# A two-layer MetaFormer block on one core: three stages in one arena, nine places of sixteen reused, 7 MB of a weight loaded in stage 1

## What is computed

```python
xn = layer_norm(_ln_c(x), norm_a, norm_b)
left  = (xn @ Wl + bl) * sigmoid(xn @ Wlg + blg)
right = (xn @ Wr + br) * sigmoid(xn @ Wrg + brg)
out_gate = sigmoid(xn @ Wog + bog)
out = einsum('bkjd,bkid->bijd', left, right) / n        # one 384x384x384 product per channel
x = x + (layer_norm(out, on_a, on_b) * out_gate) @ Wo + bo
t = tokens(x); u = _ln_t(t)
probs = softmax(u @ gate_w.T + gate_b, axis=tokens)      # 64 experts
topv, topi = top_k(probs per expert, 8)                  # 512 picks
pooled = sum over 8 picks of topv * u[topi]
h = gelu([pooled, 1] @ weight1)                          # weight1: 64 x 129 x 512
out = [h, 1] @ weight2                                   # weight2: 64 x 513 x 128
t = t + scatter_add(topi, out * topv)
```

## Time and profile before

| | before |
|---|---|
| median of three runs | 2838.45 us |
| the profiled execution, device time | 2838.67 us |
| its span, first to last instruction | 2836.9 us |
| busy in the span: PE / DVE / ACT / POOL | 2606.5 / 2388.4 / 2266.2 / 1822.3 us |
| moved by DMA | 872.97 MB, mean 308 GB/s |
| mean granted clock of TensorE | 0.979 of full speed |

### The profile page before, as it was taken

The page is one execution under the profiler, slowest core; times in us unless marked ns, Lnnn a source line. Parts: engine busy times, 40 slices in busy tenths (PEclk is TensorE's granted clock), DMA queues, the critical chain, the costliest instruction groups (busy, mean ns, idle before and its releaser), DMA issues. The chain is left out here.

```text
span 2836.9 us, 65594 instructions
## 1 busy us (share of the span) xinstructions
PE 2606.5 (92%) x15074; PEld 2134.2 (75%) x15074; DVE 2388.4 (84%) x4702; ACT 2266.2 (80%) x4430; POOL 1822.3 (64%) x1935
## 2 busy tenths in 40 slices
PE   7999999999999999899999999588899999999845
PEld 6888888888888888899999999466666666666623
DVE  6777777777777777899999999888988888898872
ACT  6888888888888888788888888578888888888840
POOL 7888888888888887200000000289999999899941
PEclk9999999999999999999999999799999999999977
DMA  5777777777777776999999999599999999999997
GB/s 196 271 271 271 270 268 270 268 266 267 270 271 270 271 269 251 339 347 352 349 348 349 349 349 350 186 362 342 344 356 349 351 350 350 344 352 346 348 336 239
DMA packets 280206, 872.97 MB, mean 308 GB/s; under 512 B 28286, under 2 KB 80656, under 8 KB 280176
## 3 DMA queue, kind: packets, MB, share of 16 engines
q1 hardware_dynamic: 276640, 871.37, 85.3%
q10 hardware_dynamic: 2896, 0.70, 0.1%
q0 software_dynamic: 640, 0.54, 0.1%
HBM read 492.97 MB, written 379.52 MB: 308 GB/s over the span
## 5 line engine op out<-in xcount | busy, mean ns | idle before, releaser
L1350 PE MATMUL banks<-x_parts,w_parts 128*128 128x512 f32 x4320 | 1067.3, 398 | 3.4 <-POOL x_parts L643 3.4
L1350 PEld LDWEIGHTS banks<-x_parts,w_parts 128*128 128x128 f32 x4320 | 791.2, 188 | 165.3 <-POOL x_parts L643 3.8
L1385 PE MATMUL banks<-left_parts,right_parts 128*128 128x384 f32 x3456 | 633.2, 340 | 21.3 <-ACT arena L881 10.2
L1385 PEld LDWEIGHTS banks<-left_parts,right_parts 128*128 128x128 f32 x3456 | 596.0, 188 | 58.3 <-issue 39.5
L1027 DVE SCALAR_TENSOR_TENSOR arena<-banks,cols,arena 128x512 f32<-128x512 f32 x576 | 406.4, 747 | 247.3 <-ACT arena L845 243.5
L946 ACT ACTIVATE work<-arena,rs 128x128 f32<-128x128 f32 x1152 | 354.4, 391 | 134.7 <-POOL rs L731 134.7
L692 POOL DMA_DIRECT2D coef<-yt x3 | 1.5, 517 | 656.2 <-DVE yt L1079 656.2
L1418 PE MATMUL banks<-wo_sb,arena 128*128 128x128 f32 x2304 | 395.0, 300 | 2.1 <-DVE arena L1146 2.1
L705 POOL TENSOR_TENSOR arena<-arena,work 128x512 f32<-128x512 f32 x288 | 359.9, 1271 | 56.7 <-DVE arena L1135 56.5
L1418 PEld LDWEIGHTS banks<-wo_sb,arena 128*128 128x128 f32 x2304 | 362.4, 193 | 35.6 <-POOL arena L705 2.9
L643 POOL TENSOR_TENSOR x_parts<-xn,x_parts 128x512 fp32r<-128x512 f32 x288 | 371.4, 1290 | 6.6 <-ACT x_parts L833 6.6
(11 more groups left out here) (209 smaller groups left out, 4270.9 us busy)
## 6 DMA issues: line engine op xcount, KB each, us to landing
arena<-in_x_dram SPq DMA_DIRECT2D x144, 512.0 KB, 3.4
left_d<-arena SPq DMA_DIRECT2D x144, 512.0 KB, 2.6
right_d<-arena SPq DMA_DIRECT2D x144, 512.0 KB, 3.4
gate_d<-arena SPq DMA_DIRECT2D x144, 512.0 KB, 4.2
arena<-right_d SPq DMA_DIRECT2D x128, 576.0 KB, 6.8
arena<-left_d SPq DMA_DIRECT2D x128, 576.0 KB, 7.9
mixed_d<-arena SPq DMA_DIRECT2D x128, 576.0 KB, 8.4
work<-mixed_d SPq DMA_DIRECT2D x144, 512.0 KB, 4.8
```

What stands on the lines that cost most here:

```text
L1350: last = nc.tensor.matmul(ps[2 + k][:, :], w_parts[:, wq, k], x_parts[:, xq, b, c], start=((wq, xq) == TERMS[0]), stop=((wq, xq) == TERMS[ ...
L1385: last = nc.tensor.matmul(ps[NT * b + t][:, 0:GRID], lr_parts[RIGHT][:, rq, b, k, t * P:(t + 1) * P], lr_parts[LEFT][:, lq, b, k], start=( ...
```

## The change

Stages 1 and 2 now lie over each other (`used[0]` is set back, so `rch2`, `lch2`, `mix` and `mixsq` take the words of x, signs, left, right and gate), within places 0 to 8; an assertion holds them there. `late_arena` moves to places 2 and 3. Places 9 to 15 are free from the start: SP loads each of these seven between two pieces of stage 1's loop, which has now eight pieces. Behind stage 3 SP loads places 4 to 8, and 2 and 3 after the last stores and transposes. ACT waits for all stores of gate before stage 2, since `mix` lies over their buffers. In stage 3 ACT's `copy_transposed` comes ahead of `normalise`.

```diff
         gate_sb = carve("b n", b=2, n=2 * CHUNK)
+        wcat = carve("k d", k=5, d=DIM)
+        used[0] = 4 * NT * GRID
+        rch2 = carve("b t n", b=2, t=NT, n=GRID)
         lch2 = carve("b t n", b=2, t=NT, n=GRID)
-        rch2 = carve("b t n", b=2, t=NT, n=GRID)
         early_words = arena[:, 0:4 * NT * GRID].rearrange("p (k b t n) -> p k b t n", k=2, b=2, t=NT)
         mix = carve("b t n", b=2, t=NT, n=GRID)
         mixsq = carve("b t n", b=2, t=NT, n=GRID)
-        wcat = carve("k d", k=5, d=DIM)
-        newton = carve("t n", t=NT, n=GRID)
         sum1 = carve("t n", t=NT, n=GRID)
         sum2 = carve("t n", t=NT, n=GRID)
+        newton = carve("t n", t=NT, n=GRID)
         rstd_map = carve("t n", t=NT, n=GRID)
...
-        assert used[0] <= W1_WORDS
+        PLACE = BANDS * HIDDEN
+        FIRST_FREE = 9
+        LATE_PLACES = (2, 3)
+        assert used[0] <= FIRST_FREE * PLACE
...
-        late_arena = arena[:, W1_WORDS - 8 * CHUNK:].rearrange("p (k b h n) -> p k b h n", k=2, b=2, h=2)
+        late_arena = arena[:, LATE_PLACES[0] * PLACE:LATE_PLACES[0] * PLACE + 8 * CHUNK].rearrange("p (k b h n) -> p k b h n", k=2, b=2, h=2)
...
-            pairs(sp, STEPS, stage1)
+            w1_view = weight1[:, 0:DIM, :].rearrange("(g j) p n -> j p g n", g=BANDS)
+
+            def load_w1(j):
+                sp.dma_start(w1_sb[:, j], w1_view[j]).then_inc(s_w1[j // 2], 16)
+
+            pairs(sp, STEPS, stage1, cuts=[lambda j=j: load_w1(j) for j in range(FIRST_FREE, SIDE)])
...
-            def load_w1(n):
-                for j in range(2 * n, 2 * n + 2):
-                    sp.dma_start(w1_sb[:, j], w1_view[j]).then_inc(s_w1[n], 16)
...
                     if isinstance(j, int) and 4 * j + r == STEPS - 2:
                         load_w1(0)
+                        load_w1(1)
...
-            for n in range(1, WLOADS - 1):
-                load_w1(n)
+            for j in range(LATE_PLACES[-1] + 1, FIRST_FREE):
+                load_w1(j)
...
-            load_w1(WLOADS - 1)
+            for j in LATE_PLACES:
+                load_w1(j)
...
+            for b in range(2):
+                act.wait_ge(s_gst[b], 16 * (STEPS // 2))
             high_halves(0, 0)
             quads(act, DIM, stage2, drain=1)
...
                         exponentials(*shifted(i, b, -4))
+                    if in_range(i, b, -2, STEPS):
+                        copy_transposed(*shifted(i, b, -2))
                     if in_range(i, b, -1, STEPS):
                         normalise(*shifted(i, b, -1))
-                    if in_range(i, b, -2, STEPS):
-                        copy_transposed(*shifted(i, b, -2))
```

More of the change, by code:

```diff
@@ L551, in store_result @@
                 sp.dma_start(out[s], late_arena[:, 1, b].rearrange("p h (c d) -> p (h c) d", c=TILES)).then_inc(s_ost[b], 16)
-            w1_view = weight1[:, 0:DIM, :].rearrange("(g j) p n -> j p g n", g=BANDS)
-            def load_w1(n):
-                for j in range(2 * n, 2 * n + 2):
-                    sp.dma_start(w1_sb[:, j], w1_view[j]).then_inc(s_w1[n], 16)
             def stage3(j):
```

## The result

The change takes **2821.61 us** (median of five runs, 2820.62 to 2821.97) against 2836.05 us for the kernel before in the same session (2833.65 to 2839.62): ratio 0.9947, interval 0.9932 to 0.9961. It is faster by 0.5%, some 15 us, where the prediction had 58 and its range ended at 2815.

What follows compares the result with a forecast made beforehand. A dependency loop among the engines in stage 3, 12.16 us per two steps, was taken as the bound, not the transfers. 2838.7 - 48.9 - 2.2 - 7.3 = 2780.3, so 2780 us; range 2758 to 2815.

Steps and rivals of the forecast that it cites:

- What is late next? I take the floors of a step one by one: Stage 3, loop broken: separate floors for engines, buffers and DMA; the buffer loop was taken as binding, 5.75 us a step.
- The term of 48.9 us: Stage 3: copy before normalise saves 0.357 us in each of 137 steady steps, reaching 5.75 us a step.
- a 12 us pair that remains: Stage 3: a sign that would show the forecast wrong, two steps still taking about 12 us.
- POOL's floor, 5.58: Stage 3: POOL's least time per step, 731.4 us busy over 131 steps, 5.58 us.
- The buffer floor of 5.68: Stage 3: a gate buffer's round of issue, landing, DVE and POOL takes 11.35 us in two steps, 5.68 each.
- The end of stage 3, -2.2: End of stage 3: with the copy first, the last logits start 2.2 us sooner.
- The gather, -7.3: After stage 3: with seven fewer weight loads there, the gather lands after 4.5 us instead of 11.78, saving 7.3 us.
- C: Stage 3 rival, chance 0.12: another way of the same length replaces the loop, only the tail gains; 2829 us, or 2836.
- B: Stage 3 rival, chance 0.20: the transfers are the wall, DVE's L1135 waits for gate loads; 2794 to 2821 us.
- D: Stage 3 rival, chance 0.04: slower, ACT's new transposes wait adds to its root wait; 6.7 us a step, 2911 us.
- E: Stage 1 rival, chance 0.04: the seven early loads stall it, with A elsewhere; 2780 + 19 = 2799 us.
- A: The main case, chance 0.60: the loop breaks, a stage 3 step takes 5.62 to 5.85 us; 2758 to 2795 us.

Runs made afterwards that it cites:

- e1: The change with the old order on ACT, normalise ahead of copy_transposed: 2828.95 us.
- e8: e5 with the old order on ACT, normalise ahead of copy_transposed: 2823.33 us.
- e3: The change, but DVE scales and adds the first tile of a step's second half itself from PSUM: 2799.75 us.
- e7: e5 with only the first half of each gate load made from step 2 on: 2782.22 us.
- e5: e3 with, in addition, POOL's copies of the best values and places moved ahead of its gate product: 2803.06 us.
- e6: e5, but SP loads the mixed values as soon as their buffer is free, ahead of its turn's other transfers: 2789.6 us.
- e11: The change with the seven early loads moved from stage 1 to behind stage 3: 2829.82 us.
- e9: e6, but POOL copies the row factors (`columns`) between its variances and its root: 2782.95 us.
- e2: The kernel before with only the new order on ACT, copy_transposed ahead of normalise: 2830.57 us.
- e10: e9 with only the first half of each gate load made from step 2 on: 2768.75 us.

## Why the prediction was wrong, point by point

- **What bounds stage 3, right.** The circle copy, logits, L1135, gate product, root, normalise, copy was the limit. e1 and e8 bring it back, and with it the wait of PE for the copy.
- **The copy ahead of normalise breaks it, right.** That wait went from 73.1 us to nothing.
- **"What is late next? I take the floors of a step one by one", wrong.** This is the step that failed. The term of 48.9 us measured 8.9. The floors of engines, buffers and the DMA said what each can do alone; I looked for no second circle among them. There was one of 12.10 us directly behind that of 12.16: POOL's copies of the best, DVE's maximum, place, addition and L1142, POOL's gate product, its root, its copies. Its members can be read from the program: `best` waits for `keep` (semaphore s_q3), and `keep` stands behind `gate` and `variances` on POOL. The wait of POOL for L1135 stood in the earlier trace rows, 50.7 us in 74 waits, and the earlier trace rows even shows it twice, 0.69 us each, 12.16 us apart. I counted it to the old loop and did not ask what else makes L1135 late. The sign that I had named for this case, a 12 us pair that remains, is the one that showed.
- **The length of DVE's addition.** I had no term for it. It took 369 ns on average before and 598 after, since its new place in time falls on POOL's L716: 0.23 us a step that no count of instructions shows. (The 271 in the expectation of e3 is its length when nothing holds it, not the average before.)
- **POOL's floor, 5.58, too low.** It was busy time alone. The root waits 0.28 us for the variances whenever nothing stands between them: 5.79 a step in e7, and my 5.75 could not have been reached in this order of POOL, whatever the buffers did.
- **The buffer floor of 5.68 and the landing of 7.4 us.** In e5, where DVE waits for these loads, a step took about 5.98 us, 127 gate loads in 760 us (47.8 us of waits, a landing after 7.5 us), so 11.35 us for two steps was too short as well; the landing of 7.5 accounts for only 0.1 of the missing 0.6, and where the rest lies is open. With the mixed values out of the gate loads' way (e6) a step became 5.80, and there POOL is full: 722.6 us busy and 35.7 waiting for its own variances, of 760.
- **The end of stage 3, -2.2: -1.6. The gather, -7.3: -6.4.** The mechanism holds: e11 has everything but the early loads, and its gather takes 13.31 us.
- **Stage 1, the stores of gate, the places: 0 and 0.3 us measured**, as forecast.
- **The rivals.** Of their figures C's 2829 came nearest to the result of 2821.6, and its sentence came true: another way of nearly the same length replaces the loop. But stage 3 did gain 8.9 us, which C had at nothing. The way I named, normalise late to the transposes, was not it. B was not reached by the change, with 1.4 us of waits for transfers, though 2821.6 lies at the slow end of its times: a time alone would not have told B from C. Its sign, DVE waiting for gate loads, appears in e3 to e6 and in e9, but the rate goes higher than I put it: 370 GB/s at share 0.99 in e9, not 363 at share 1. D and E didn't happen: both waits of ACT together shrank, from 119.5 to 95.1 us for the root, and the list of waits has none of ACT for the transposes.
- **The rule of about 358 GB/s** that I cited from the Trainium skill (DMA: Bandwidth & Descriptors, Bandwidth) does not bind here: e9 held 370 over 760 us of mixed traffic. The figure that the same section gives for a core that streams alone, 425, is not reached in any stretch shown here.
- **The chances.** 0.60 on A rested on the floors being complete. With one loop traced out of several it should have been C's chance that was large, and the low end of the gain should have been inside the range. The lower end of the range, 2758, doesn't quite follow from my own bounds either: 2838.7 - 66.7 - 2.8 - 9.5 is 2759.7.

## What to carry to other kernels

When an edit breaks a dependency loop, trace the next one before costing the gain with busy times: go through each wait that is left in the rows, follow what makes its releaser late until the circle closes, and include the small instructions by which a slow engine hands a buffer back. An engine's floor is its busy time plus the waits it has for its own results. An edit may also be worth little only because another limit of nearly the same length stands beside it: the reordering here was worth 6 us alone and 20 us once POOL's copies and DVE's addition were moved (e8 against e5).

## What the runs showed of the hardware

- An fp32 addition of 128x128 on DVE with both inputs in SBUF took 0.27 us alone and 0.92 us when POOL's `tensor_tensor` of 128x384 had begun 0.22 us before it; the longest in the change's 800 us took 1.07 us. The same sum, scaled, with one input in PSUM took 0.33 us on average in e3. The other way round, with DVE first by 0.15 us or more, POOL's instruction kept its 1.00 us; with DVE first by 0.05 to 0.08 us, as in 58 steps of the 800 us before, POOL's took 1.04 to 1.09 us.
- A gather of four times 128 rows landed 11.8 to 13.3 us after its last issue in the three kernels that issue twelve loads of the first weight behind stage 3 (before, e2, e11), and after 5.0 to 6.5 us in every run with only five there. With the order alone changed (e2) it was 13.15 instead of 11.78; why it grew is open.
- Seven loads of 1 MB between pieces of a loop in which the DMA was busy 0.72 of the time cost PE nothing: it was busy 1126.0 of the first 1145 us without them (e11) and 1125.5 with them (the change).
- Halving one of a step's three loads of 512 KB shortened the landing of the stores too, from 6.1 us (e5) to 3.4 us (e7), though the step got shorter; from e9 to e10 it went from 5.8 to 4.0 us.
